# ScalarE evaluates one 128x1 Silu, Exp and Gelu ahead of three stages of a two-layer attention and mixture kernel

## The reference

```python
x = x + _L0_xattn_ref(_layernorm(x), ctx_1024, ctx_1024, mask, ...)   # 16 heads, softmax
x = x + _L0_ffn_ref(_layernorm(x), ...)    # hidden = silu(x @ wg.T) * (x @ wu.T); 8 experts, top 2, inner width 1024
x = x + _L1_xattn_ref(_layernorm(x), ctx_1024, ctx_1024, fside, fside, fside, ...)   # one head, softmax
x = x + _L1_ffn_ref(_layernorm(x), ...)    # h = gelu(inp) * gate; 8 experts, top 2, inner width 512
```

## Time and profile before

| What | us |
|---|---|
| median of three executions | 883.07 |
| all three | 883.07, 890.54, 882.83 |
| span of the profiled execution, first to last instruction | 889.0 |
| PE busy / PEld busy | 700.3 / 550.1 |
| DVE busy | 547.8 |
| ACT busy | 403.1 |
| POOL busy | 302.8 |

### The profile page before, as it was taken

How to read it: one execution, slowest core, us unless ns; L and a number is a source line. 1 busy time by engine, 2 the same in 40 slices (tenths; PEclk the granted TensorE clock), 3 DMA queues, 4 the chain that set the end, 5 groups by cost and what they waited for, 6 DMA issues and landing times.

```text
span 889.0 us, 19049 instructions
## 1 busy us (share of the span) xinstructions
PE 700.3 (79%) x6278; PEld 550.1 (62%) x6278; DVE 547.8 (62%) x1322; ACT 403.1 (45%) x720; POOL 302.8 (34%) x306
## 2 busy tenths in 40 slices
PE   5476796989564799999999899996862098898981
PEld 4232454555354688888897798895531087777771
DVE  7768576887836545647556656547696446566441
ACT  1135466576513434646545555442552044546331
POOL 7505301416337422222121131232167414334342
PEclk9689799989776799999999999997875599999996
DMA  4562300601524542536344643425022555464332
GB/s 140 118 141 51 59 2 24 180 24 49 153 81 151 185 129 36 165 51 171 78 126 98 170 112 101 107 39 179 25 101 95 174 170 131 115 147 114 63 55 40
DMA packets 68418, 92.24 MB, mean 104 GB/s; under 512 B 14442, under 2 KB 54435, under 8 KB 68348
## 3 DMA queue, kind: packets, MB, share of 16 engines
q1 hardware_dynamic: 41788, 63.37, 24.1%
q0 software_dynamic: 14592, 16.24, 10.6%
q10 hardware_dynamic: 11968, 11.72, 5.3%
HBM read 64.21 MB, written 29.87 MB: 106 GB/s over the span
## 4 chain that ended last, share of the span: by engine, by line
PE 48%; DVE 18%; issue 11%; ACT 9%; POOL 5%; DMA 5%; ACTq 2%; another core or an unknown queue 1%; DVEq 0%; POOLq 0%; SPq 0%
PE ps L685 45%; POOL rows L631 3%; DVE probs L1726 3%; DVE mx L1591 2%; DMA out_x<-keys,row_to 2%; DVE keys L1804 2%; DMA probs<-rows 2%; ACT probs L1189 1%; ACT probs L1271 1%; ACT expo L1186 1%; DVE keys L1783 1%; ACT probs L1267 1%; PE ps L933 1%; DVE stats L1383 1%; ACTq L1252 1%
## 5 line engine op out<-in xcount | busy, mean ns | idle before, releaser
L1804 DVE TENSOR_TENSOR keys<-probs,ps 128x512 f32<-128x512 f32 x122 | 82.8, 687 | 177.3 <-ACT probs L1267 86.3
L685 PE MATMUL ps<-keys,slot 128*128 128x256 f16 (+1 forms) x1440 | 146.5, 263 | 5.4 <-DVE keys L1783 2.7
L685 PE MATMUL ps<-keys,probs 128*128 128x256 f16 (+1 forms) x1488 | 139.5, 255 | 5.1 <-DVE probs L1405 3.7
L685 PEld LDWEIGHTS ps<-keys,slot 128*128 128x128 f16 x1440 | 127.8, 99 | 22.8 <-issue 5.4
L685 PEld LDWEIGHTS ps<-keys,probs 128*128 128x128 f16 x1488 | 124.2, 98 | 19.0 <-issue 7.2
L575 POOL DMA_INDIRECT attended<-keys,row_to x42 | 67.2, 1601 | 166.0 <-ACT keys L1280 142.2
L1267 ACT ACTIVATE probs<-ps 128x512 f32<-128x512 f32 x122 | 71.4, 598 | 65.9 <-PE ps L685 63.7
L1280 ACT ACTIVATE keys<-ps,carried 128x256 f32<-128x256 f32 x80 | 33.5, 470 | 117.9 <-POOLq L580 41.6
L1809 DVE TENSOR_TENSOR probs<-keys,probs 128x512 f16<-128x512 f32 x122 | 83.3, 688 | 3.6 <-ACT probs L1271 1.9
L1271 ACT CAST probs<-keys 128x512 f16<-128x512 f32 x122 | 74.8, 614 | 22.0 <-DVE keys L1804 21.9
L1726 DVE TENSOR_TENSOR probs<-expo,probs 128x512 f16<-128x512 f32 x80 | 61.1, 775 | 34.1 <-ACT probs L1189 28.2
(11 more groups left out here) (285 smaller groups left out, 1145.7 us busy)
## 6 DMA issues: line engine op xcount, KB each, us to landing
inbox<-in_W SPq DMA_DIRECT2D x24, 512.0 KB, 3.9
probs<-rows ACTq DMA_DIRECT2D x44, 260.0 KB
inbox<-in_wg SPq DMA_DIRECT2D x16, 512.0 KB, 5.2
inbox<-in_wu SPq DMA_DIRECT2D x16, 512.0 KB, 3.7
inbox<-in_wd SPq DMA_DIRECT2D x16, 512.0 KB, 4.2
rows<-zeros SPq DMA_DIRECT2D x16, 260.0 KB
x<-in_x SPq DMA_DIRECT2D x4, 512.0 KB, 6.1
q_out<-queries SPq DMA_DIRECT2D x8, 256.0 KB, 2.1
```

Of the source, the lines that this page charges most:

```text
L685: return pe.matmul(o, l, r, start=start, stop=stop, **kw)
L1804: dve.tensor_tensor(h32[:, j % 2, :], s_act[:, j % 2, :], ps[:, 2 * (j % 2) + 1, :], ALU.mult).then_inc(S(r + "_h32"), 1)
```

## The change

A new 128x1 tile `ready` and a helper `load_table(function)` are added. The helper emits one ACTIVATE of the given function, from a column of the constant tile `mean` into `ready`. Nothing reads `ready`, and no semaphore is touched. The helper is called in three places on ScalarE: as the first thing of `experts(l)` in both mixtures, with Silu and with Gelu, and behind the weight casts that follow the first mixture, with Exp.

```diff
+        ready = sb("ready", [P, 1])
         stats = sb("stats", [P, 3 * GT, 6])
...
+            def load_table(function):
+
+                act.activation(ready[:, :], mean[:, 0:1], function)
+
             def experts(l):
                 r, pairs = l.r, l.pairs
+                load_table(l.act)
                 act.sem_inc(S(r + "_y"), 1)
                 act.sem_inc(S(r + "_added"), 1)
                 act.wait_ge(S(r + "_table"), 1)
...
             experts(L[0])
             for n in range(len(L[1].chunks)):
                 high_part(L[1], 0, 0, n)
+            load_table(ACT.Exp)
```

## The result

The changed kernel takes 880.19 us (median of 12 executions, 878.89 to 883.00), the kernel before 884.45 us (12 executions, 882.78 to 890.54, the three of the forecast among them). The ratio is 0.9948, with a 95% interval from 0.9931 to 0.9964: some 4.6 us faster. The forecast was 880.4 us, within 1% of the time before, and 2.7 us off the median then known. Two later comparisons of the same pair gave 0.9959 (0.9943 to 0.9974) and 0.9958 (0.9932 to 0.9984).

The account below looks back on a forecast made before the run. TensorE bounds the kernel (48% of the chain), so only loads it waits for count: 2.54 (loop) + 0 + 0.17 (second attention) + 0 - 0 = 2.71 us off 883.07, giving 880.4 us, range 878.0 to 888.0.

Parts of the forecast that it names:

- The loop's two passes: First mixture's loop, second and third pass: TensorE's 1.27 us stand at the table load goes in each, 2.54 us together.
- The sum: All terms, 2.54 + 0 + 0.17 + 0 - 0 = 2.71 us, taken off the median of 883.07 us, giving 880.4 us.
- the control: A block of the loop's first pass without a table load: TensorE runs 96 matmuls in 10.65 us without a gap.
- The wait for the weights: First mixture, TensorE's 3.70 us wait at 492.12 for the next expert's weights: fetches start 1.27 us earlier, its length stays.
- the rival of no gain or half of it: Weights' DMA sets the pace, so the 3.70 us wait grows; 1.4 or 0.2 us left, 881.6 to 882.9 us; chance 0.14.
- The first pass: First mixture's loop, first pass: removing its load gains 0, as slow-clocked TensorE hid it; bounds 0 and 1.28 us.
- The second attention: Load ahead of the second attention's Exp: moving it gains 0.17 us, limited by VectorE's 0.19 us wait for ScalarE's cast.
- the bound of 0.57: Most the second attention's term could gain: 0.57 us, the time TensorE waited for the Exp.
- The Gelu and the additions: Second mixture's first Gelu load: gain 0, bounds 0 and 1.28 us; three moved loads and tiny ACTIVATEs in idle time: cost 0.
- The price of a load: A load costs its 1.28 us record, not the Trainium skill's 2.66 us per switch, which would give about 877.6 us.
- the 1%: Whole kernel's time: about 1% (8.8 us) is what a measurement can tell from no change.
- The slower rival: TensorE's clock falls in the first mixture, or the median lands on slow executions, 887.8 us; chance 0.19.

Follow-up runs that it names:

- e4: The kernel before, unchanged, run and traced a second time: 883.61 us, ratio 0.9985 against other executions of the same program.
- e10: The kernel before, unchanged, traced a third time: 884.61 us, ratio 1.0001.
- e5: The changed kernel as it is, run and traced again: 881.89 us against 883.47 for the kernel before, ratio 0.9959.
- e11: The changed kernel as it is, traced a third time: 879.56 us, ratio 0.9958 to the kernel before.
- e3: Changed kernel with its three added ACTIVATEs using Identity, which needs no table, so all loads stay in their old places: 883.17 us, ratio 0.9999 to the kernel before.
- e6: Changed kernel plus a tiny Exp before four first-mixture Silus, exposing two table loads each time: 893.44 us, ratio 1.0103 to the kernel before.
- e7: Changed kernel plus a tiny Exp and Silu in 14 first-mixture blocks, 28 loads in ScalarE's idle time: 880.27 us, ratio 0.9975 to the kernel before.

## Why the prediction was right

**The loop's two passes: right, 2.54 us forecast.** The stands are there in each trace of a kernel with the loads in the loop, and in none without. TensorE's 96 matmuls took 12.09 to 12.10 us with the load, in both passes, and 10.80 to 10.83 without. It arrives at the end of the stage: from the scaling of block 0 to that of block 20, the last, the first mixture takes 287.37 and 287.36 us in e4 and e10, and 284.87 in both e5 and e11. In all four the clock fell at block 13, and the difference is 2.5 us. The sum had found just 0.01 us to spare, and that shows: 10.82 us are still 0.17 more than the control's 10.65. The 48th and 49th matmul start 0.25 to 0.28 us apart, the others at most 0.12, a short stop that the rows don't mark.

**The wait for the weights: right.** It is 3.71 us after 3.70, and in the later traces 3.83 and 3.80 after 3.90 and 3.71. The fetches moved with the rest, and the rival of no gain or half of it falls.

**The first pass: right, 0.** The load's removal brings no shorter first block: its 96 matmuls take 12.25 to 13.32 us in the five traces with the load and 12.46 to 13.48 in the six without. The kernels with the load have no wait there above 0.18 us (e3).

**The second attention: right in size, with two wrong steps inside.** The term was 0.17 us, and 0.29 us was measured in the first pair (5.27 to 4.98 us). One step took VectorE's marked idle of 0.19 us as all there was. But without a wait the low part also starts before the instruction ahead of it on VectorE has ended. That one is, before:

```profile
629.08 0.17 DVE L1867 TENSOR_SCALAR mx<-mx 128x4 f32<-128x4 f32 x1
```

From its start to that of the low part, 629.44 - 629.08 = 0.36 us became 619.36 - 619.28 = 0.08 us. The other step was that TensorE gains its 0.57 us. It holds where the maximum is computed early, with its last instruction 0.2 to 0.3 us behind the scores' start. In e4 and e10 of the kernel before, and in e5 and e11 of the changed one, it starts 0.88 to 0.92 us behind. Then the Exp can move only from 1.26 us behind the scores' start to 1.12 and 1.08, TensorE keeps most of its wait, and the low part starts after 5.12 and 5.08 us where it was 5.26 and 5.27, so 0.14 to 0.19 us earlier. TensorE in e5:

```profile
618.24 0.66 PE L1059 MATMUL ps<-ident,expo 128*128 128x128 f32 x4 [0.43 <-ACT expo L1336]
```

All of this is within the bound of 0.57.

**The Gelu and the additions: right, 0.** The second Gelu waits for TensorE still, and the tiny ACTIVATEs of 203 ns lie under more than 5 us of idle time each. What the additions cost is 0, but the prediction had no term for the shift, which gives the 0.2 us of e3.

**The price of a load: right.** 1.28 us and nothing around it, by e6. It costs what TensorE waits, by e7: 28 loads that TensorE did not wait for cost nothing, within 1.8 us.

**The sum: 2.7 us forecast, 3.6 us measured with 0.7 to either side over all executions, 4.6 us in the first comparison.** By the terms as measured it is 2.5 us in the loop, 0.14 to 0.29 in the second attention and 0.2 near the end, so 2.9 to 3.0 us. The rest, some 0.6 us, lies within the spread, and I can't place it. A candidate is the clock behind the wait at block 13: 2.7 us when it falls. It was spared more often in the kernels without the loads, but eleven traces don't decide whether that is more than chance. That the forecast of 880.4 us came within 0.2 us of the measured 880.19 is partly luck: it was taken off a median of three executions, and that of twelve lay 1.4 us higher, so the first comparison measured a larger gain than the forecast one. And the 1% that the prediction gives as the least that can be told from no change was too wide: twelve executions against twelve give 0.17% to either side.

**The slower rival: its mechanism exists, at another length.** A stand of 2.77 us brought the clock down afterwards each time it was tried; those of 1.27 us, which the change removed, never did. Nothing was to be won or lost there by this change. The rival's time of 887.8 us, which stood for the slowest executions, did not appear: the changed kernel's 32 executions lie between 876.5 and 883.9 us.

## What to carry to other kernels

Look in the compiled list for where the compiler put each ACT_TABLE_LOAD. Behind a stand-alone wait it starts only when its function's input is there, and in a loop it is repeated in each pass although the table is already in place. A tiny ACTIVATE of the coming function, in idle time ahead of the loop or stage, takes it off the path. Its worth is what the bounding engine is seen to wait at that place, here 1.27 us at two of five loads, and not the number of loads times their length.

## What the runs showed of the hardware

A table load takes 1283 ns in each of the traces, with 0.01 us to the ACTIVATE behind it, and ScalarE's queue can issue a DMA during it (e7, 349.27 us). TensorE's clock was at 1.2 GHz for 2.6 us and more behind a stand of 2.77 us, in a stage where it had been busy before, four times of four; it was at 2.4 GHz behind ten stands of 1.26 to 1.28 us and two of 2.40 and 2.41. Behind the wait of 3.7 to 3.9 us for weights the clock fell in some executions and not in others, without a change of the program: the changed kernel's 96 matmuls there took 10.65 us in one trace and 13.38 in another. Three 128x1 ACTIVATEs more, ahead of three stages, made one gap of ScalarE near the program's end 0.2 us shorter, with table loads in them or not (e3). And one execution of the kernel before had the last Silu of each of its partial blocks 0.36 us late, which no other trace repeated.
